# First factors of down's adapters as fp32 products of the unsplit gated tokens

## The reference

```python
def lora_add(base, inp, A, B):
    Ab = A[layer_idx][lora_indices]
    Bb = B[layer_idx][lora_indices]
    t = jnp.einsum('bri,bni->bnr', Ab, inp)
    return base + jnp.einsum('bor,bnr->bno', Bb, t) * SCALE
gate = lora_add(jnp.einsum('bnh,fh->bnf', x, W_gate), x, A_gate, B_gate)
up = lora_add(jnp.einsum('bnh,fh->bnf', x, W_up), x, A_up, B_up)
act = jax.nn.silu(gate) * up
down = lora_add(jnp.einsum('bnf,hf->bnh', act, W_down), act, A_down, B_down)
```

## Time and profile before

| | |
|---|---|
| median of 3 runs | 635.57 us (635.55 to 635.84) |
| the profiled execution | 635.31 us |
| its span, first to last instruction | 633.7 us |
| PE busy | 623.4 us, 98% |
| DVE busy | 451.9 us, 71% |
| ACT busy | 318.6 us, 50% |
| POOL busy | 245.0 us, 39% |
| PE's share of the chain that ended last | 84% |
| granted clock of PE | 1.00 |

### The profile page before, as it was taken

How to read it: one execution, slowest core, us unless ns; L and a number is a source line. 1 busy time by engine, 2 the same in 40 slices (tenths; PEclk the granted TensorE clock), 3 DMA queues, 4 the chain that set the end, 5 groups by cost and what they waited for, 6 DMA issues and landing times.

```text
span 633.7 us, 8018 instructions
## 1 busy us (share of the span) xinstructions
PE 623.4 (98%) x2920; PEld 502.7 (79%) x2920; DVE 451.9 (71%) x547; ACT 318.6 (50%) x427; POOL 245.0 (39%) x197
## 2 busy tenths in 40 slices
PE   8999999999999999999999999999999999999996
PEld 6788888888778876778787787878787888788885
DVE  4475745344477998885447888745679998999987
ACT  5676526144635344442113444425557887478860
POOL 3580020000000006752023666440003898959986
PEclk9999999999999999999999999999999999999999
DMA  8651031201022102311102100252222212322203
GB/s 251 169 151 36 26 116 58 67 0 46 21 72 68 33 34 69 130 59 58 35 33 100 34 33 31 65 108 56 90 68 99 63 58 64 100 67 71 79 1 132
DMA packets 24474, 45.18 MB, mean 71 GB/s; under 512 B 9973, under 2 KB 12021, under 8 KB 24373
## 3 DMA queue, kind: packets, MB, share of 16 engines
q1 hardware_dynamic: 21972, 40.80, 20.9%
q0 software_dynamic: 2176, 3.36, 2.0%
q10 hardware_dynamic: 288, 0.52, 0.2%
HBM read 40.74 MB, written 2.10 MB: 68 GB/s over the span
## 4 chain that ended last, share of the span: by engine, by line
PE 84%; DVE 5%; ACT 3%; issue 3%; DMA 2%; POOL 1%; SPq 1%; DVEq 0%
PE ps_down L1830 7%; PE ps_down L1831 7%; PE ps_down L1832 7%; PE ps_up L1830 4%; PE ps_up L1831 4%; PE ps_up L1832 4%; PE ps_m L2019 3%; PE ps_m L2020 3%; PE ps_up L2019 3%; PE ps_gate L2019 3%; PE ps_down L2019 3%; PE ps_down L2020 3%; PE ps_up L2020 3%; PE ps_gate L2020 3%; PE ps_gate L1831 3%; PE ps_gate L1830 3%
## 5 line engine op out<-in xcount | busy, mean ns | idle before, releaser
L817 POOL TENSOR_TENSOR act_lo<-up,act_hi 128x512 fp32r<-128x512 f32 x14 | 18.2, 1299 | 199.0 <-ACT act_hi L1085 199.0
L1830 PE MATMUL ps_down<-act_hi,w_hi 128*128 128x512 f32 (+1 forms) x180 | 71.0, 394 | 0.0
L1831 PE MATMUL ps_down<-act_lo,w_hi 128*128 128x512 f32 (+1 forms) x180 | 70.3, 391 | 0.0
L1832 PE MATMUL ps_down<-act_hi,w_lo 128*128 128x512 f32 (+1 forms) x180 | 70.1, 389 | 0.0
L848 POOL TENSOR_TENSOR up_sum<-up_sum,up_more 128x1024 f32<-128x1024 f32 x14 | 33.8, 2413 | 64.4 <-DVE up_more L1405 64.4
L1296 DVE TENSOR_TENSOR w_lo<-w_raw,w_hi 128x512 fp32r<-128x512 f32 (+4 forms) x41 | 44.4, 1083 | 18.8 <-ACT w_hi L919 14.1
L919 ACT ACTIVATE w_hi<-w_raw 128x1024 fp32r<-128x1024 f32 (+4 forms) x30 | 27.0, 900 | 46.3 <-DVE w_raw L1303 22.0
L1830 PEld LDWEIGHTS ps_down<-act_hi,w_hi 128*128 128x128 f32 (+1 forms) x180 | 33.8, 188 | 7.4
L1832 PEld LDWEIGHTS ps_down<-act_hi,w_lo 128*128 128x128 f32 (+1 forms) x180 | 33.8, 188 | 7.2
L1831 PEld LDWEIGHTS ps_down<-act_lo,w_hi 128*128 128x128 f32 (+1 forms) x180 | 33.8, 188 | 6.7
L1296 DVE TENSOR_TENSOR b_rows<-b_raw,b_hi 32x1024 fp32r<-32x1024 f32 (+2 forms) x23 | 25.4, 1104 | 19.2 <-ACT b_rows L937 12.0
(11 more groups left out here) (289 smaller groups left out, 1823.8 us busy)
## 6 DMA issues: line engine op xcount, KB each, us to landing
w_int<-in_ffn_gu SPq DMA_DIRECT2D x14, 512.0 KB, 3.5
w_raw<-in_cond_gu SPq DMA_DIRECT2D x9, 512.0 KB, 3.4
w_raw<-in_ffn_gu SPq DMA_DIRECT2D x9, 512.0 KB, 3.5
w_raw<-in_ffn_dn SPq DMA_DIRECT2D x8, 448.0 KB, 3.2
w_int<-in_ffn_dn SPq DMA_DIRECT2D x8, 448.0 KB, 3.2
xp<-in_x SPq DMA_DIRECT2D x8, 256.0 KB, 5.1
w_raw_third<-in_ffn_gu SPq DMA_DIRECT2D x4, 512.0 KB, 3.9
xp<-in_x SPq DMA_DIRECT2D x1, 2048.0 KB, 10.1
```

The source lines that it names most:

```text
L1830: nc.tensor.matmul(ps[0:m, :], w_hi[0:r, s, cols], rhs_hi(k, r), start=start and n == 0, stop=False)
L1831: nc.tensor.matmul(ps[0:m, :], w_hi[0:r, s, cols], rhs_lo(k, r), start=False, stop=False)
L1832: last = nc.tensor.matmul(ps[0:m, :], w_lo[0:r, s, cols], rhs_hi(k, r), start=False, stop=stop and n == len(ks) - 1)
```

## The change

The first factors of down are kept in fp32, unsplit, and multiplied with the gated products themselves before these are split, a pair of samples at a time as for gate/up. Two tiles are done at a time: tiles 0 and 1 behind the first gate sums of tile 2, tiles 2 and 3 behind those of tile 4, tiles 4 and 5 behind `cond down a`, 6 and 7 in tile 8, 8 and 9 in tile 10, and tile 10 in `cond down b` between the base sums of the two halves. Odd tiles get a place of their own for the gated products. One DVE operation now scales and masks all of t of down; its splits follow at once, and `first_weights` comes behind them. The factors are ordered by two DVE copies behind tile 0 instead of being split behind tile 3, and POOL loads them before it waits for `t_sums`. `adapter_t`, `sums_and_more`, `hi_of_a_dn` and `lo_of_a_dn` go.

```diff
@@ places
+        gated_odd = [place(f"gated_odd{part}", [P, CH, CT], F32, x) for part, x in enumerate((at["act_hi"] + 24 * KB, at["act_lo"] + 20 * KB))]
-        a_dn = place("a_dn", [P, NKD, CH, 2 * RB], F32R, at["lora0"])
+        a_dn = place("a_dn", [P, NKD, NB, R], F32, at["lora0"])
+        a_dn_raw = place("a_dn_raw", [P, NB, NKD * R], F32, at["lora0"] + 4 * NKD * NB * R)
-        a_dn_raw = place("a_dn_raw", [P, NB, NKD * R], F32, at["xp"])
...
+        def gated_of(ph, j):
+
+            return gated_odd[ph.part] if j % 2 else gated
@@ POOL
             pool.wait_ge(start_lo, len(start))
-            pool.wait_ge(t_sums, CH)
             for b in range(NB):
...
+            pool.wait_ge(t_sums, CH)
             nc.gpsimd.memset(pack_raw[:, :], 0.0).then_inc(pack_zero, 1)
@@ ACT
+            def hi_of_t_down():
+
+                act.wait_ge(t_masked, CH + 1)
+                nc.scalar.activation(t_hi[:, 0, 0:PT], gated[:, 0, 0:PT], ACT.Copy).then_inc(t_hi_done, 1)
+                for c in range(CH):
+                    for pair in (2 * c, 2 * c + 1):
+                        for row in (0, 1):
+                            last = nc.scalar.activation(t_rows[quarter(row), 0, pair_tokens(pair)], gated[quarter(pair), 0, 0:PT], ACT.Copy)
+                    last.then_inc(t_hi_rows, 1)
...
-                    if not isinstance(i, int) or n >= CH:
-                        act.wait_ge(act_ready, n - 1)
-                    nc.scalar.activation(gated[0:m, c, :], unit_banks(ph, i, jj, c)[0][0:m, :], ACT.Silu).then_inc(silu_done, 1)
+                    tile = ph.first + 2 * i + jj
+                    if tile > 1:
+                        act.wait_ge(act_ready, n - 3)
+                        act.wait_ge(t_read, tile - 1)
+                    nc.scalar.activation(gated_of(ph, 2 * i + jj)[0:m, c, :], unit_banks(ph, i, jj, c)[0][0:m, :], ACT.Silu).then_inc(silu_done, 1)
...
+            def small_t(ph):
+
+                if ph.name == "cond down b":
+                    hi_of_t_down()
+                    for piece in range(2):
+                        piece_hi(named["ffn0 gate/up a"], 0, piece)
+                    return
...
-                    if ph is phases[0] and j == 3:
-                        hi_of_a_dn()
@@ DVE
+            def lo_of_t_down():
+
+                dve.wait_ge(t_hi_done, CH + 1)
+                for c in range(CH):
+                    for pair in (2 * c, 2 * c + 1):
+                        for row in (2, 3):
+                            last = lo(t_rows[quarter(row), 0, pair_tokens(pair)], gated[quarter(pair), 0, 0:PT], t_hi[quarter(pair), 0, 0:PT])
+                    last.then_inc(t_lo_rows_done, 1)
...
+            def order_a_dn():
+
+                dve.wait_ge(a_dn_in, 16 * 2 * NB)
+                for rows, k0, k1 in ((P, 0, NKD - 1), (F0_TAIL, NKD - 1, NKD)):
+                    nc.vector.tensor_copy(a_dn[0:rows, k0:k1, :, :],
+                                          a_dn_raw[0:rows, :, k0 * R:k1 * R].rearrange("p b (k r) -> p k b r", r=R)).then_inc(a_dn_ready, 1)
...
+            def small_t(ph):
+
+                if ph.name == "cond down b":
+                    dve.wait_ge(t_read, NKD)
+                    nc.vector.scalar_tensor_tensor(out=gated[:, 0, 0:PT], in0=ps_m[:, 0:PT], scalar=0.5, in1=seg_mask[:, :],
+                                                   op0=ALU.mult, op1=ALU.mult).then_inc(t_masked, 1)
+                    lo_of_t_down()
+                    first_weights(named["ffn0 gate/up a"])
+                    return
...
-                    if ph is phases[0] and j == 3:
-                        lo_of_a_dn()
+                    if ph is phases[0] and j == 0:
+                        order_a_dn()
@@ PE, gate_up_tile
                         last.then_inc(ready, 1)
+                        if g == 0 and c == 0 and 2 * i + jj in (2, 4):
+                            for j in (2 * i + jj - 2, 2 * i + jj - 1):
+                                t_down(ph, j)
@@ PE
+            def t_down(ph, j):
+
+                tile, rows = ph.first + j, P if ph.first + j < NKD - 1 else F0_TAIL
+                pe.wait_ge(a_dn_ready, 2)
+                pe.wait_ge(prod_done, CH * (min(tile | 1, NKD - 1) + 1))
+                for pair in range(PAIRS):
+                    factors = a_dn[0:rows, tile, 2 * pair:2 * pair + 2, :].rearrange("p b r -> p (b r)")
+                    last = nc.tensor.matmul(ps_m[quarter(pair), 0:PT], factors, gated_of(ph, j)[0:rows, pair // 2, pair_tokens(pair % 2)],
+                                            start=tile == 0, stop=tile == NKD - 1)
+                last.then_inc(t_read, 1)
...
                     if ph.name == "cond down b" and 2 * i + jj == 1:
-                        pe.wait_ge(t_added, CH)
+                        pe.wait_ge(t_masked, CH + 1)
                         scales(following[ph], 0, 1)
...
                     if o == 0:
 
+                        down_base(ph, o, 0).then_inc(base_done, 1)
                         if ph.name == "cond1":
-                            down_base(ph, o, 0).then_inc(base_done, 1)
-                        t_of(ph, 0)
-                        if ph.name != "cond1":
-                            down_base(ph, o, 0).then_inc(base_done, 1)
-                        t_of(ph, 1)
+                            for c in range(CH):
+                                t_of(ph, c)
+                        else:
+                            t_down(named["cond gate/up b"], NKD - CUT - 1)
                         down_base(ph, o, 1).then_inc(base_done, 1)
                         return
...
                 if ph.name == "cond down a":
-                    for c in range(CH):
-                        t_down(ph, c)
+                    for j in (CUT - 2, CUT - 1):
+                        t_down(phases[0], j)
```

More of the change, by code:

```diff
@@ L993, in gate_up_hi @@
                 nc.scalar.activation(act_hi[0:m, ds(2 * i + jj, 1), chunk(c)].rearrange("p a n -> p (a n)"),
-                                     gated[0:m, c, :], ACT.Copy).then_inc(act_hi_done, 1)
+                                     gated_of(ph, 2 * i + jj)[0:m, c, :], ACT.Copy).then_inc(act_hi_done, 1)
             def unit_silu(u):
@@ L1139, in down_tile @@
                         nc.scalar.activation(y_hi[:, o, chunk(c)], gated[:, c, :], ACT.Copy).then_inc(h_hi_done, 1)
-            def small_t(base, scale):
-                for c in range(CH):
[L1144 to L1150, removed]
+            def small_t(ph):
[4 more added lines that the diff above has]
+                    return
+                for c in range(CH):
+                    act.wait_ge(t_sums, CH + c + 1)
+                    nc.scalar.activation(gated[0:RB, c, 0:PT], ps_m[RB:2 * RB, pair_sums(c)], ACT.Copy, scale=2.0).then_inc(t_lo_rows, 1)
                 for c in range(CH):
-                    hi_of_t(base, c, 1)
+                    hi_of_t(c, 1)
             act.wait_ge(warm_zero, 1)
@@ L1661, in down_tile @@
                         lo(y_lo[:, o, chunk(c)], gated[:, c, :], y_hi[:, o, chunk(c)]).then_inc(h_ready, 1)
-            def small_t(base, scale):
-                n = base - CH
-                for c in range(CH):
-                    dve.wait_ge(t_lo_rows, n + c + 1)
-                    for rows, _, cols in sums_and_more(base, c):
-                        here = gated[rows, c, 0:PT]
-                        last = nc.vector.scalar_tensor_tensor(out=here, in0=ps_m[rows, cols], scalar=scale, in1=here, op0=ALU.mult, op1=ALU.add)
-                    last.then_inc(t_added, 1)
-                    dve.wait_ge(t_added, n + c + 1)
-                    nc.vector.tensor_tensor(gated[0:RB, c, 0:PT], gated[0:RB, c, 0:PT], seg_mask[0:RB, :], ALU.mult).then_inc(t_masked, 1)
-                    if base == CH and c == 0:
-                        first_weights(named["ffn0 gate/up a"])
+            def small_t(ph):
[6 more added lines that the diff above has]
+                    return
+                for c in range(CH):
+                    here = gated[0:RB, c, 0:PT]
+                    dve.wait_ge(t_lo_rows, c + 1)
+                    nc.vector.scalar_tensor_tensor(out=here, in0=ps_m[0:RB, pair_sums(c)], scalar=2.0, in1=here, op0=ALU.mult, op1=ALU.add).then_inc(t_added, 1)
+                    dve.wait_ge(t_added, c + 1)
+                    nc.vector.tensor_tensor(here, here, seg_mask[0:RB, :], ALU.mult).then_inc(t_masked, 1)
                 for c in range(CH):
-                    lo_of_t(base, c, 1)
+                    lo_of_t(c, 1)
             nc.vector.memset(warm[:, :].bitcast(F32), 0.0).then_inc(warm_zero, 1)
@@ L1855, in pair_factors @@
                 return factors[:, sample:sample + 2, :].rearrange("p b r -> p (b r)")
-            def adapter_t(c, a_cols, ks, rhs_hi, rhs_lo, rows=lambda k: P, start=True, stop=True):
-                last = None
-                for n, k in enumerate(ks):
-                    r = rows(k)
```

(17 more changed lines are left out.)

44 lines of the change are left out of this document (14 added, 30 removed).

## The result

| | before | after |
|---|---|---|
| median | 635.59 us (635.06 to 635.84, 6 executions) | 638.29 us (636.58 to 639.78, 6 executions) |
| ratio, 95% interval | | 1.0046 [1.0029, 1.0064] |
| the profiled execution | 635.31 us | 636.58 us |
| its span | 633.7 us | 635.0 us |
| PE busy | 623.4 us | 620.7 us |

The change makes the kernel slower by 2.7 us, 0.46%. The forecast was 636.5 us, with 0.54 on a time within 0.2% of before. The profiled execution is the fastest of the six, and the forecast for it, 636.3, was close. The other five are 638.28, 638.29, 638.30, 639.70 and 639.78. So two questions are left: whether the sum is right term by term, and what adds 1.7 us to three of the others and 3.2 us to two.

What follows compares the result with a forecast made beforehand. PE, busy 623.4 of 633.7 us, was taken to bound the kernel. Net PE work of -3.3 us and stalls of 2.2 and 2.1 came, phase by phase, to +1.0: 636.3 profiled, 636.5 us median, range 634.9 to 638.5.

Steps and rivals of the forecast that it cites:

- rival (d): PE's clock falls in a pause; some microseconds at half speed give 639 to 640 us; chance 0.03.
- The sum: Whole kernel: runs, stalls and removed products add to +1.0 us, taking the profiled execution from 635.31 to 636.3 us.
- a run of eight: Eight fp32 products for two tiles on PE: 8 x 0.108 plus 0.33 for entering and leaving the form, 1.19 us.
- The run of four for tile 10: Four fp32 products in `cond down b`, between the base sums of the two halves: 0.76 us of PE.
- The whole saving of 3.3 us: Net PE work: six fp32 runs add 6.7 us, the 44 products of `t_down` that go save 10.0.
- the 14 us of the prediction's estimate: If fp32's four passes ran one after another, 44 products take 18.8 us, making the change some 14 us dearer.
- The copies of `order_a_dn`: Two DVE copies behind tile 0, ahead of a split: 1.0 us, range 0.9 to 1.7.
- rival (b): Copies run at two-input pace, or a run between adapter products costs 0.5: +0.7 to +1.0, 637.3 us; chance 0.13.
- The first stall: PE waits near 38.4, behind tile 2's gate sums, for DVE's product of tile 1: 2.2 us.
- The second: PE waits before `scales` near 190 in `cond down b` for DVE's `first_weights` product: 2.1 us (1.6 to 2.5).
- Rival (a): The loads of a_dn come late, adding 1 to 2 us: 637.5 to 638.5 us; chance 0.2.
- the bound that was given for it: Start phase: a_dn loads move closer to the token and factor row copies PE waits on; costed 0, bound 0 to 0.5.

Runs made afterwards that it cites:

- the four other traces: Changed kernel with first run later (636.36 us) or `first_weights` product ahead of the mask (635.64); kernel before with only an added 2.2 us (639.69) or 2.9 us pause (640.03).
- the kernel with both edits: Changed kernel with tiles 0 and 1's products behind tile 2's up sums and the `first_weights` product ahead of t's mask: 632.18 us, ratio 0.9948.
- the one with the first run later: Changed kernel with the products of tiles 0 and 1 behind the up sums of tile 2's first half instead of its gate sums: 636.36 us, ratio 1.0007.
- the middle pause: Kernel before with only a PE wait for tile 1's first `act_lo` added behind tile 2's first-half gate sums, 2.2 us: 639.69 us, ratio 1.0047.
- A pause of 1.5 us: Kernel before with only a PE wait for both products of tile 1 added behind tile 2's first-half gate sums: 637.28 us, ratio 1.0019.

## Why the prediction was wrong

**The step that failed: rival (d).** The text gave it a chance of 0.03 and said "I don't expect it in pauses of 2.2 us", because PE works 0.76 of 5.70 us at the end and the granted clock still averages 0.96. That row can't carry this, and read in shorter stretches it shows the opposite (profile of before; PE's last matmul ends at 628.8):

```profile
632.00:633.00 1.00, 0.00 (x0) 0.00 (x0) 0.00 (x0) 0.00 (x0) 0.00 (x0) 1.00 0.00 0
633.00:633.70 0.70, 0.00 (x0) 0.00 (x0) 0.00 (x0) 0.00 (x0) 0.00 (x0) 0.68 0.00 0
```

The clock does fall when PE stands still. It falls some microseconds late, here after 633, so that a mean from 628 on hides it, and at the end of the kernel it costs nothing. In the middle of the kernel PE is busy again when it comes, and pays. The price that the text named (639 to 640) was near the truth for a fall behind each of the two stalls; its chance was not. Of the twelve executions of the kernel after, two have the time without a fall, seven are about one fall above it and three at least two: some 13 falls in 24 stalls, if each step of the times is a fall. That is a rough count, since 638.29 has the clock of an execution without a fall and the start phase can add as much. And both profiles of the kernel after are of executions without a fall; the falls themselves are seen only in the four other traces, each with a single stall.

**The sum was right, as a sum for an execution without a fall.** It gave +1.0 us for the profiled execution; measured +1.27 (636.58 against 635.31). Its terms:

- The products: a run of eight was put at 1.19 us. At tile 4 the adapters start at 65.26, the run at 65.58 and the next plain matmuls at 66.58 and, after its longer step of 0.34, 66.92: 0.32 + 1.34 less two steps of 0.227 is 1.21. The run of four for tile 10, put at 0.76, comes to 0.78 in the same way in `cond down b` (187.60, 187.92, 188.49, 188.83). The whole saving of 3.3 us shows in the kernel with both edits, 3.1. The Trainium skill ("FP8 and Floating Point Precision", TensorE Precision Notes) gives a true fp32 product four passes. Had they cost the change the 14 us of the prediction's estimate, the kernel with both edits could not be 3.5 us faster than before; a run of eight at 1.21 us agrees with four passes only if the four column blocks work side by side, since at that estimate (0.43 us a product) eight one after another would take 3.4 us.
- The copies of `order_a_dn`: 1.0 us, measured 0.96. The Trainium skill ("VectorE: DVE Perf Modes", The perf-mode tier table) has such copies at twice the two-input rate; the row agrees, while the upper bound of 1.7 and with it half of rival (b) falls.
- The first stall: 2.2, measured 2.04, from 38.5 to 40.55. Together with its run it moved the up sums by 3.3 us (38.57 to 41.88), where the terms had 2.2 + 1.19 = 3.4. The second: 2.1, measured 2.19. Its chain (run, mask, copy, eight splits, product) came out as written: mask product at 188.62, splits 3.46 us, product 3.5 us behind their start.
- No stall at tiles 4, 8 and 10 or behind `cond down a`: no such line in PE's waits.
- The `scales` ahead of `cond down b` start at 183.67, 2.81 us after their time before; the terms had 2.71. `cond down b` as a phase came out at -1.5 instead of -1.7: the split at 203.40 stood at 202.13 before, 1.27 later, and 1.27 less 2.81 is -1.54. These two small misses, 0.1 and 0.2, are the 0.27 between 1.0 and 1.27.

**Rival (a)** did not happen: POOL's first load went out at 19.61 instead of the 20.0 assumed, and DVE's copies had no wait for them. The dearer wait for `b_rows`, 0.5 instead of 0.3 us, is within the bound that was given for it, and it is open whether the earlier loads are its cause: the profile with both edits shows 0.3 again with the same loads, the one with the first run later 1.0.

**The miss in numbers.** The median of 638.29 is the 636.6 of an execution without a fall plus 1.7, about one fall. The forecast of 636.5 missed it by 1.8 us: one fall, 1.6, and 0.2 of other things. The term that the sum put at nothing is the fall of the clock behind each stall.

## What to carry to other kernels

On a PE that is busy throughout, price a new stall of about 2 us at its length plus a likely fall of the clock, some 1.6 us here, and doubt a profile whose execution is the fastest of its kernel: it shows the stalls and hides the falls. Look at the times of all executions; steps between them are a sign, and a trace of a slower execution is the proof. Read a clock over stretches of a microsecond or two, not as a mean over a stretch in which the engine mostly stands. Where a product must wait for another engine, put it where its input is long ready, and on the engine that feeds PE do first what PE waits for: these two moves turned +2.6 us into -3.5 (638.22 and 632.18 against 635.66, on one chip).

## What the hardware showed that I had not expected

- PE's granted clock goes from 1.00 to 0.50 and back within a few microseconds behind a single stall (waits of 1.9 to 2.7 us in the four traces) in an otherwise full stream, and not in every execution. Ahead of the stall PE had run without a wait, since the one for `b_rows` at 34 to 35 us or for longer. The matmuls of 512 columns then start every 0.43 us instead of 0.23 for about 3 us. The Trainium skill ("TensorE: Matmul & The Clock Gate", Part 1) says that idle time brings the engine to its lower level; the traces agree with that for these stalls, in part of the executions; the profiles of the kernel after, with waits of 2.0 and 2.2 us and a clock of 1.00 behind both, are the other part.
- The low stretch is not in the stall, and in three of four cases not right behind it: PE resumes at full pace for 1.1 us (the middle pause, 41.02 to 42.12) to 1.9 us (192.90 to 194.76) and slows then; behind the first stall of the change the clock fell within the run, 0.3 us after it began at 40.16. Counted from the last matmul ahead of the stall, the fall came 2.2 to 4.0 us later in the four traces, and 4.5 us after PE's last matmul at the end of the kernel before.
- Four traces with a fall, at two places, with fp32 products or plain sums behind it, give 1.58, 1.58, 1.60 and 1.59 us: the price of a fall is steady, only whether it comes is not. A pause of 1.5 us had a median of just its own length over before, 1.6 us. What decides in one execution whether the clock falls stays open.
